# Second expert layer: one sum in DRAM, its accumulating scatters one at a time, copied straight to the output

## The chip, the cores and the metric

The kernel runs on one core of a Trainium2 chip. The metric is the device time of one execution in microseconds (us); lower is better. All spans below are from the first to the last instruction of that core.

## What is computed

A two-layer transformer on `x` of 2048 tokens by 128 channels, in f32. Layer 0 is an attention and a mixture of 64 experts, layer 1 is a lookup in place of attention and a mixture of 8 experts with two experts for each token. The change touches only the last of these:

```python
def _L1_ffn_ref(hidden_states, gate_w, gate_up_proj, down_proj):
    ...
    probs = jax.nn.softmax(x @ gate_w.T, axis=-1)
    w, idx = jax.lax.top_k(probs, TOP_K)              # TOP_K = 2 of E = 8
    w = w / jnp.sum(w, axis=-1, keepdims=True)
    combine = jnp.zeros((T, E), x.dtype).at[jnp.arange(T)[:, None], idx].add(w)
    def step(acc, inputs):
        gup, dn, ce = inputs
        g, u = jnp.split(x @ gup.T, 2, axis=-1)
        acc = acc + ce[:, None] * (jax.nn.silu(g) * u @ dn.T)
        return (acc, None)
...
x = x + _L1_ffn_ref(_layernorm(x, axis=-1), ...)
```

Each token's output row is its residual row `x` plus two weighted expert rows.

## The kernel before

The program is written by hand, engine by engine, with semaphores: SP issues the plain DMAs, PE multiplies, DVE and ACT move and transform, POOL (GpSimd) multiplies by masks in layer 0 and issues all indirect DMAs. Each engine and each queue runs its instructions in the order in which they are written.

The second expert layer is sparse. 4096 pairs of token and expert are sorted into slots of `slots_dram`, expert by expert, each expert's share filled up to whole tiles of 128 slots. There are at most 39 tiles (`TILES1`), and all 39 are always worked. A slot's row holds the normalised token (128 values), the number of its token (column `P`) and what gives its weight. An empty slot holds zeros and the number of a spare row behind the 2048 tokens.

- POOL L922 scatters the token rows into `slots_dram` (32 indirect DMAs).
- SP L378 loads tile j into `XG[j % 8]`. From tile 8 on it first waits until the scatter that read this buffer has landed (`summed0` or `summed1`, L377).
- PE turns the tile (L667), DVE copies it to `XTT` (L1226), ACT copies the expert's weights to `WB` (L825), PE multiplies gate and up (L679, 16 products of 128x128 by 128x128), ACT and DVE make the hidden values (L835, L1246), PE multiplies down (L689), and DVE weights the result into `YO[j % 4]` (`y_out`, L1233), which raises `y_taken`. From tile 4 on, `y_out` first waits until scatter j - 4 has landed (L1232).
- POOL L929 issues one indirect DMA for each tile: it adds the 128 rows of `YO` to the rows of a sum in DRAM that the token numbers name. There are two sums, `sums_dram[0]` for even tiles and `sums_dram[1]` for odd ones, each of 2048 + 128 rows. Scatter j waits for `y_taken` (L926) and for the landing of scatter j - 2 (L928), the last one on the same sum, since one token may occur in two tiles.
- Sum 0 starts as the residual `X` (SP L372, 1 MB, after the lookup), sum 1 as zeros (SP L326, 1088 KB, at the start of the program).
- At the end SP waits for both sums (L381), loads both in four quarters (L385, eight DMAs of 256 KB) into `X` and `BS`, DVE adds them quarter by quarter (L1258), and SP stores each quarter to `out` (L389).

The tiles on PE, DVE and ACT run some tiles ahead of the scatters, as far as `XG` (8), `YO` (4) and the pairs of other buffers allow.

Of the kernel before, what the change touches and what calls it, by code (L numbers as in the profile page):

```python
# [12 lines left out]
P = 128  # L13
T = 2048
NT = T // P
BANK = 512
CH = 512
NC = T // CH
# [14 lines left out]
TILES1 = (T * TOP1 + E1 * (P - 1)) // P  # L33
NXG = 8
# [73 lines left out]
def build(nc, a, out):  # L108

    f32, bf16, f32r, i32 = mybir.dt.float32, mybir.dt.bfloat16, mybir.dt.float32r, mybir.dt.int32  # L110
    ALU, ACT, AX = mybir.AluOpType, mybir.ActivationFunctionType, mybir.AxisListType
# [1 line left out]

    mask0_dram = nc.dram_tensor("mask0_scratch", (E0, T), f32, kind="Internal").ap()
    slots_dram = nc.dram_tensor("slots_scratch", (TILES1 * P, XW), f32, kind="Internal").ap()
    sums_dram = [nc.dram_tensor(f"sums_scratch{i}", (T + P, P), f32, kind="Internal").ap() for i in range(2)]

    ctx = ExitStack()
    with ctx:
        def sb(name, shape, dt=f32, stack=ctx):  # L120
            return stack.enter_context(nc.sbuf_tensor(name, shape, dt))
# [3 lines left out]
        def sem(name):  # L125
            if name not in sems:
                sems[name] = ctx.enter_context(nc.semaphore(name))
            return sems[name]
# [4 lines left out]
        X = sb("X", [P, NT, P])  # L133
# [22 lines left out]
        padrow = sb("padrow", [P, XW])  # L156
# [80 lines left out]
        sparse = ExitStack()  # L237
# [5 lines left out]
        YO = [sb(f"YO{i}", [P, P], f32, sparse) for i in range(4)]  # L243
        hits = sb("hits", [P, 2, E1], f32, sparse)
        wslot = sb("wslot", [P, 4], f32, sparse)
        BS = sb("BS", [P, NT, P], f32, sparse)
        sparse.close()

        lk = ExitStack()
# [52 lines left out]
        @block.sync  # L302
        def _(sp):
            def load(dst, src, name="loaded"):
                sp.dma_start(dst, src).then_inc(sem(name), 16)

            load(X[:, :, :], a["x"].rearrange("(t p) c -> p t c", p=P), "x_loaded")
            load(CF[:, :], a["consts"][:, 0:NF], "cf_loaded")
            load(YT[:, 0:NB], a["consts"][:, NF:NF + NB], "cb_loaded")
            load(wqk[:, :, :], a["wqk"], "qkv_loaded")  # L310
            load(bqk[:, :], a["bqk"], "qkv_loaded")
            load(wvt[:, :], a["wvt"], "qkv_loaded")
            load(bvb[:, :], a["bv"].partition_broadcast(P), "qkv_loaded")
            load(gam[:, :], a["gamma"].partition_broadcast(P), "rest_loaded")
            load(gw0[:, :], a["gw0"], "rest_loaded")
            load(gb0[:, :], a["gb0"].partition_broadcast(P), "rest_loaded")
            load(wol[:, :], a["wol"], "rest_loaded")
            load(bol[:, :], a["bol"].partition_broadcast(P), "rest_loaded")
            load(wout[:, :], a["wout"], "rest_loaded")
            load(boutb[:, :], a["bout"].partition_broadcast(P), "rest_loaded")  # L320
            load(gw1[:, :], a["gw1"], "rest_loaded")

            sp.wait_ge(sem("pad_ready"), 2)
            sp.dma_start(slots_dram.rearrange("(j p) c -> p j c", p=P),
                         padrow[:, :].unsqueeze(1).to_broadcast([P, TILES1, XW])).then_inc(sem("padded"), 16)
            sp.dma_start(sums_dram[1].rearrange("(t p) c -> p t c", p=P),  # L326
                         padrow[:, 0:P].unsqueeze(1).to_broadcast([P, NT + 1, P])).then_inc(sem("padded"), 16)
            sp.dma_start(sums_dram[0][T:T + P, :], padrow[:, 0:P]).then_inc(sem("padded"), 16)

            def load_weights(l, it, h, weights):  # L330
                sub = MOE[l]["sub"]
                sp.dma_start(WR[:, h * sub:(h + 1) * sub, :], weights[ds(it * 2 + h, 1)].squeeze(0)).then_inc(
                    sem(f"w_loaded{l}_{h}"), 16)

            def load_masks(l, it, h, mask_dram):
                k = it * 2 + h
                for s, p0, p1, e in SEGMENTS0:
                    sp.dma_start(MK[p0:p1, h, s, :], mask_dram[ds(k * 4 + e, 1), :].to_broadcast([p1 - p0, T])
                                 ).then_inc(sem(f"m_loaded{l}_{h}"), 16)

            def moe_loads(l, weights, mask_dram):

                m = MOE[l]
                sub, nb, npro, n = m["sub"], m["n_body"], m["n_pro"], m["halves"] // 2
                load_masks(l, 0, 0, mask_dram)
                load_masks(l, 0, 1, mask_dram)
                with sp.Fori(1, n) as it:
                    for h in range(2):
                        sp.wait_ge(sem(f"w_split{l}_{h}"), it * sub)
                        load_weights(l, it, h, weights)  # L350
                    for h in range(2):

                        sp.wait_ge(sem(f"h_ready{l}"), npro + (it - 1) * nb + (h + 1) * nb // 2)
                        load_masks(l, it, h, mask_dram)

                sp.sem_inc(sem(f"w_loaded{l}_0"), 16)


            sp.dma_start(WR[:, 2 * SUB0 - 2:2 * SUB0, :], a["wsh"]).then_inc(sem("wsh_loaded"), 16)
            load_weights(0, 0, 0, a["w0"])  # L360
            sp.wait_ge(sem("wsh_split"), 2)
            load_weights(0, 0, 1, a["w0"])
            sp.wait_ge(sem("mask_t0"), 4)
            sp.dma_start(mask0_dram[:, :], MT[0:E0, :]).then_inc(sem("mask_stored0"), 16)
            sp.wait_ge(sem("mask_stored0"), 16)
            moe_loads(0, a["w0"], mask0_dram)

            sp.wait_ge(sem("x_moe0"), NC)
            load(W1GU[:, :, :], a["w1gu"], "w1_loaded")
            load(W1D[:, :, :, :], a["w1d"], "w1_loaded")  # L370
            sp.wait_ge(sem("x_lookup"), 1)
            sp.dma_start(sums_dram[0][0:T, :].rearrange("(t p) c -> p t c", p=P), X[:, :, :]).then_inc(sem("x_kept"), 16)  # L372

            sp.wait_ge(sem("dispatched"), 16 * NT * TOP1)
            for j in range(TILES1):
                if j >= NXG:
                    sp.wait_ge(sem(f"summed{j % 2}"), 16 * ((j - NXG) // 2 + 1))  # L377
                sp.dma_start(XG[j % NXG][:, :], slots_dram[j * P:(j + 1) * P, :]).then_inc(sem(f"xg_loaded{j % NXG}"), 16)  # L378

            for i in range(2):  # L380
                sp.wait_ge(sem(f"summed{i}"), 16 * ((TILES1 + 1 - i) // 2))  # L381
            for q in range(NC):
                rows = slice(q * CH, (q + 1) * CH)
                for i, dst in ((0, X), (1, BS)):
                    sp.dma_start(dst[:, 4 * q:4 * q + 4, :], sums_dram[i][rows, :].rearrange("(t p) c -> p t c", p=P)  # L385
                                 ).then_inc(sem(f"sums_back{q}"), 16)
            for q in range(NC):
                sp.wait_ge(sem("x_final"), q + 1)
                sp.dma_start(out[q * CH:(q + 1) * CH, :].rearrange("(t p) c -> p t c", p=P),  # L389
                             X[:, 4 * q:4 * q + 4, :]).then_inc(sem("stored"), 16)  # L390
            sp.wait_ge(sem("stored"), 16 * NC)


# [447 lines left out]
        def _(pool):  # L841
# [72 lines left out]
                             ALU.add).then_inc(sem("xs_ready"), 1)  # L914
            norm_scale(3)

            pool.wait_ge(sem("padded"), 48)
            pool.wait_ge(sem("x_kept"), 16)
            pool.wait_ge(sem("rows_ready"), 3)
            for t in range(NT):  # L920
# [3 lines left out]

            for j in range(TILES1):
                pool.wait_ge(sem("y_taken"), j + 1)  # L926
                if j >= 2:
                    pool.wait_ge(sem(f"summed{j % 2}"), 16 * (j // 2))  # L928
                gp.indirect_dma_start(sums_dram[j % 2][:, :],  # L929
                                      bass.IndirectOffsetOnAxis(ap=XG[j % NXG][:, P:P + 1].bitcast(i32), axis=0),  # L930
                                      YO[j % 4][:, :], None, compute_op=ALU.add).then_inc(sem(f"summed{j % 2}"), 16)


        @block.vector
        def _(dve):
# [292 lines left out]
            def y_out(j):  # L1228

                dve.wait_ge(sem("y_done"), j + 1)  # L1230
                if j >= 4:
                    dve.wait_ge(sem(f"summed{j % 2}"), 16 * ((j - 4) // 2 + 1))  # L1232
                TS_(YO[j % 4][:, :], PS[:, (6 + j % 2) * BANK:(6 + j % 2) * BANK + P], wslot[:, j % 4:j % 4 + 1], None,  # L1233
                    ALU.mult).then_inc(sem("y_taken"), 1)

# [17 lines left out]
                    y_out(j - 1)  # L1253
            dve.wait_ge(sem("slot_weight"), TILES1)
            y_out(TILES1 - 1)
            for q in range(NC):
                dve.wait_ge(sem(f"sums_back{q}"), 32)
                TT(X[:, 4 * q:4 * q + 4, :], X[:, 4 * q:4 * q + 4, :], BS[:, 4 * q:4 * q + 4, :], ALU.add).then_inc(  # L1258
                    sem("x_final"), 1)


_OUT_SHAPE = (1, T, P)
# [54 lines left out]
```

## Time and profile before

| | us |
|---|---|
| three runs | 1236.63, 1236.97, 1242.84; median 1236.97 |
| the profiled execution's own time | 1237.94 |
| its span | 1236.1 |
| PE / DVE / ACT / POOL busy in it | 993.0 / 854.4 / 628.0 / 489.4 |
| scatters of the last stage, first to last start | 1114.94 to 1219.76, 39 of them |
| last landing to the end of the span | 1223.0 to 1236.1 |

The profile is one execution. Starts are counted from the start of the span. POOL's "busy" for an indirect DMA is the time in which it makes the descriptors; the transfer itself follows. When a transfer has landed is seen from the row of whoever waited for it.

### The profile page before, as it was taken

To read this page: it belongs to the slowest core of one execution; us is meant where nothing else is said; L and a number is where in the kernel's file an instruction comes from. 1 tells how busy PE (TensorE), PEld (TensorE's weight loads), DVE (VectorE), ACT (ScalarE), POOL (GpSimd) and SP (SyncE) were. 2 spreads that over 40 slices of the span, in tenths; PEclk is the share of its full clock that TensorE was granted. 3 is DMA by queue.
4 is the path that set the end of the run, shared out by engine and by line. 5 is a ranking of instruction groups with operands and counts; after the bars stand their busy time and mean duration, and the time that the engine had idled before them with its cause. 6 is when DMAs were issued, how large, how long until landed. Compare 5 with 4: busy or idle time off the path is not lost.

```text
span 1236.1 us, 18848 instructions
## 1 busy us (share of the span) xinstructions
PE 993.0 (80%) x6540; PEld 621.8 (50%) x6540; DVE 854.4 (69%) x1310; ACT 628.0 (51%) x839; POOL 489.4 (40%) x346
## 2 busy tenths in 40 slices
PE   4344999999999935999999999999963675029993
PEld 2112222222222324877777777777743335029993
DVE  5789999999999865776677767776766334204442
ACT  1330888888888721555655555555531100115551
POOL 4000000000000041788888888888851001545553
PEclk9655999999999967999999999999985576559997
DMA  5600000000000003657564576545313001123335
GB/s 135 124 1 1 1 2 1 2 1 2 1 2 2 1 20 85 156 126 185 138 156 121 135 178 142 149 121 142 81 68 136 0 1 34 36 60 45 51 52 117
DMA packets 41101, 86.87 MB, mean 70 GB/s; under 512 B 5009, under 2 KB 30993, under 8 KB 34577
## 3 DMA queue, kind: packets, MB, share of 16 engines
q1 hardware_dynamic: 34400, 81.11, 26.0%
q0 software_dynamic: 6640, 4.94, 2.9%
q8 instruction: 41, 0.67, 0.2%
q14 instruction: 20, 0.16, 0.0%
HBM read 74.40 MB, written 11.63 MB: 70 GB/s over the span
## 4 chain that ended last, share of the span: by engine, by line
PE 42%; POOL 20%; DVE 17%; issue 12%; ACT 6%; DMA 2%; POOLq 1%; SPq 0%; ACTq 0%; DVEq 0%
POOL HF L894 14%; PE PS L499 11%; PE PS L486 6%; PE PS L476 6%; PE PS L679 6%; DVE HL L1091 4%; PE PS L689 3%; POOL slots_scratch L922 2%; POOL WL L863 2%; ACT HH L776 2%; DVE small L1011 1%; DVE hm L994 1%; ACT PB L744 1%; PE PS L417 1%; DVE XN L953 1%
## 5 line engine op out<-in xcount | busy, mean ns | idle before, releaser
L744 ACT ACTIVATE PB<-PS 128x1024 f32<-128x1024 f32 x256 | 261.8, 1024 | 92.0 <-PE PS L486 81.9
L1032 DVE TENSOR_SCALAR PS<-PS 128x1024 f32<-128x1024 f32 x256 | 302.7, 1228 | 7.6 <-PE PS L476 2.7
L894 POOL TENSOR_TENSOR HF<-SU,MK 128x512 f32<-128x512 f32 x192 | 283.6, 1497 | 60.1 <-DVE SU L1098 60.1
L1091 DVE TENSOR_TENSOR HL<-HF,HH 128x512 fp32r<-128x512 f32 x200 | 188.4, 942 | 119.0 <-ACT HH L776 118.7
L846 POOL TENSOR_SCALAR rstd<-moments 128x16 f32<-128x16 f32 x4 | 1.0, 261 | 535.9 <-DVE moments L949 535.9
L776 ACT CAST HH<-HF 128x512 fp32r<-128x512 f32 x200 | 124.2, 621 | 168.0 <-POOL HF L894 155.7
L499 PE MATMUL PS<-PB,VS 128*32 128x256 f32 x2048 | 164.3, 393 | 0.6 <-ACT PB L744 0.5
L567 PE MATMUL PS<-XH,WL 128*128 128x512 f32 x400 | 162.3, 406 | 0.0
L569 PE MATMUL PS<-XH,WH 128*128 128x512 f32 x400 | 157.5, 394 | 0.0
L568 PE MATMUL PS<-XL,WH 128*128 128x512 f32 x400 | 156.6, 391 | 0.0
L1098 DVE TENSOR_TENSOR SU<-PS,SL 128x512 f32<-128x512 f32 x200 | 135.7, 678 | 13.0 <-ACT SL L783 12.9
L783 ACT ACTIVATE SL<-PS 128x512 f32<-128x512 f32 x200 | 118.7, 593 | 37.1 <-PE PS L569 36.1
L476 PE MATMUL PS<-QS,KP 64*128 64x512 bf16 x512 | 100.1, 388 | 5.1 <-DVE QM L1028 2.9
L486 PE MATMUL PS<-QM,KP 64*128 64x512 bf16 x512 | 100.9, 391 | 1.0 <-DVE PS L1032 0.9
L567 PEld LDWEIGHTS PS<-XH,WL 128*128 128x128 f32 x400 | 75.0, 188 | 33.4 <-DVE SU L1098 15.5
L929 POOL DMA_INDIRECT sums_scratch<-YO,XG x39 | 60.8, 1558 | 59.3 <-DVE YO L1233 56.8
L569 PEld LDWEIGHTS PS<-XH,WH 128*128 128x128 f32 x400 | 75.2, 188 | 17.9
L551 PE MATMUL PS<-HL,WH 128*128 128x512 f32 x200 | 82.5, 413 | 1.1 <-DVE HL L1091 1.1
L568 PEld LDWEIGHTS PS<-XL,WH 128*128 128x128 f32 x400 | 75.3, 188 | 13.7
L549 PE MATMUL PS<-HH,WL 128*128 128x512 f32 x200 | 79.1, 396 | 1.0 <-ACT HH L776 1.0
L1226 DVE COPY XTT<-PS 128x128 f32<-128x128 f32 x39 | 11.4, 292 | 98.6 <-PE PS L667 53.1
L552 PE MATMUL PS<-HH,WH 128*128 128x512 f32 x200 | 79.1, 396 | 0.0
(212 smaller groups left out, 1253.7 us busy)
## 6 DMA issues: line engine op xcount, KB each, us to landing
MK<-mask_scratch SPq DMA_DIRECT2D x32, 768.0 KB, 11.8
MK<-mask_scratch SPq DMA_DIRECT2D x32, 512.0 KB, 9.2
WR<-in_w SPq DMA_DIRECT2D x16, 576.0 KB, 4.5
MK<-mask_scratch SPq DMA_DIRECT2D x32, 256.0 KB, 9.8
W1GU<-in_w1gu SPq DMA_DIRECT2D x1, 4096.0 KB, 12.1
slots_scratch<-padrow SPq DMA_DIRECT2D x1, 2827.5 KB, 20.2
XG<-slots_scratch SPq DMA_DIRECT2D x39, 72.5 KB, 1.9
W1D<-in_w1d SPq DMA_DIRECT2D x1, 2048.0 KB, 17.3
```

What stands on the lines that cost most here:

```text
L476: last = mm(bank(2 * (u % 3) + k), KP[g][hp][r, n * P:(n + 1) * P], QS[g][r, c * CH:(c + 1) * CH], start=True, stop=True)
L486: last = mm(bank(2 * (u % 3) + k), KP[g][hp][r, n * P:(n + 1) * P], QM[g][r, c * CH:(c + 1) * CH], start=False, stop=True, skip_group_chec ...
L499: last = mm(PS[32 * j:32 * j + 32, at + q.start:at + q.stop], VS[:, n, g * HG + j, :], PB[u // 2 % 3][:, 2 * (j % 2) + j // 2, q], start=( ...
L567: mm(o, WL[:, slot, w], XH[:, x], start=True, stop=False)
L568: mm(o, WH[:, slot, w], XL[:, x], start=False, stop=False)
L569: last = mm(o, WH[:, slot, w], XH[:, x], start=False, stop=True)
L744: A(PB[u // 2 % 3][:, 2 * hp:2 * hp + 2, :], pair_banks(u).rearrange("p (j q) -> p j q", j=2), ACT.Exp).then_inc(sem("exp_done"), 1)
L776: nc.scalar.copy(HH[buf][:, :], HF[buf % 2][:, :]).then_inc(sem(f"hh_ready{l}"), 1)
L894: ins = gp.tensor_tensor(HF[k % 2][:, :], SU[k % 2][:, :], mask, ALU.mult)
L1032: TS_(pair_banks(u), pair_banks(u), 4.0, 0.0, ALU.mult, ALU.max).then_inc(sem("relu_done"), 1)
L1091: TT(HL[buf][:, :], HF[buf % 2][:, :], HH[buf][:, :].bitcast(f32), ALU.subtract).then_inc(sem(f"hl_ready{l}"), 1)
L1098: TT(SU[k % 2][:, :], bank(2 * (k % 2) + 1), SL[k % 2][:, :], ALU.mult).then_inc(sem(f"su_done{l}"), 1)
```

## The change

Both sums become one, `sums_dram`, with 2048 + 128 rows that start as the residual `X`. Its scatters share one semaphore, `summed`, and scatter j waits for the landing of scatter j - 1 rather than of scatter j - 2. The zeroing of sum 1 and its buffer `BS` go. At the end neither loads nor additions are left: after the last scatter has landed, SP issues four DMAs from the sum in DRAM straight to `out` in DRAM.

```diff
-    sums_dram = [nc.dram_tensor(f"sums_scratch{i}", (T + P, P), f32, kind="Internal").ap() for i in range(2)]
+    sums_dram = nc.dram_tensor("sums_scratch", (T + P, P), f32, kind="Internal").ap()
...
-        BS = sb("BS", [P, NT, P], f32, sparse)
...
-            sp.dma_start(sums_dram[1].rearrange("(t p) c -> p t c", p=P),
-                         padrow[:, 0:P].unsqueeze(1).to_broadcast([P, NT + 1, P])).then_inc(sem("padded"), 16)
-            sp.dma_start(sums_dram[0][T:T + P, :], padrow[:, 0:P]).then_inc(sem("padded"), 16)
+            sp.dma_start(sums_dram[T:T + P, :], padrow[:, 0:P]).then_inc(sem("padded"), 16)
...
-            sp.dma_start(sums_dram[0][0:T, :].rearrange("(t p) c -> p t c", p=P), X[:, :, :]).then_inc(sem("x_kept"), 16)
+            sp.dma_start(sums_dram[0:T, :].rearrange("(t p) c -> p t c", p=P), X[:, :, :]).then_inc(sem("x_kept"), 16)
...
                 if j >= NXG:
-                    sp.wait_ge(sem(f"summed{j % 2}"), 16 * ((j - NXG) // 2 + 1))
+                    sp.wait_ge(sem("summed"), 16 * (j - NXG + 1))
...
-            for i in range(2):
-                sp.wait_ge(sem(f"summed{i}"), 16 * ((TILES1 + 1 - i) // 2))
+            sp.wait_ge(sem("summed"), 16 * TILES1)
             for q in range(NC):
                 rows = slice(q * CH, (q + 1) * CH)
-                for i, dst in ((0, X), (1, BS)):
-                    sp.dma_start(dst[:, 4 * q:4 * q + 4, :], sums_dram[i][rows, :].rearrange("(t p) c -> p t c", p=P)
-                                 ).then_inc(sem(f"sums_back{q}"), 16)
-            for q in range(NC):
-                sp.wait_ge(sem("x_final"), q + 1)
-                sp.dma_start(out[q * CH:(q + 1) * CH, :].rearrange("(t p) c -> p t c", p=P),
-                             X[:, 4 * q:4 * q + 4, :]).then_inc(sem("stored"), 16)
+                sp.dma_start(out[rows, :], sums_dram[rows, :]).then_inc(sem("stored"), 16)
...
-            pool.wait_ge(sem("padded"), 48)
+            pool.wait_ge(sem("padded"), 32)
...
                 pool.wait_ge(sem("y_taken"), j + 1)
-                if j >= 2:
-                    pool.wait_ge(sem(f"summed{j % 2}"), 16 * (j // 2))
-                gp.indirect_dma_start(sums_dram[j % 2][:, :],
+                if j >= 1:
+                    pool.wait_ge(sem("summed"), 16 * j)
+                gp.indirect_dma_start(sums_dram[:, :],
...
-                                      YO[j % 4][:, :], None, compute_op=ALU.add).then_inc(sem(f"summed{j % 2}"), 16)
+                                      YO[j % 4][:, :], None, compute_op=ALU.add).then_inc(sem("summed"), 16)
...
                 if j >= 4:
-                    dve.wait_ge(sem(f"summed{j % 2}"), 16 * ((j - 4) // 2 + 1))
+                    dve.wait_ge(sem("summed"), 16 * (j - 3))
...
-            for q in range(NC):
-                dve.wait_ge(sem(f"sums_back{q}"), 32)
-                TT(X[:, 4 * q:4 * q + 4, :], X[:, 4 * q:4 * q + 4, :], BS[:, 4 * q:4 * q + 4, :], ALU.add).then_inc(
-                    sem("x_final"), 1)
```

No instruction changes its place on PE or ACT. On POOL's queue, the first scatters of the second expert layer stand like this before (out<-in with buffer numbers, then what each waits for):

```order
L929 DMA sums_scratch0<-YO0,XG0 2176x128 [waits y_taken]
L929 DMA sums_scratch1<-YO1,XG1 2176x128 [waits y_taken]
L929 DMA sums_scratch0<-YO2,XG2 2176x128 [waits summed0,y_taken]
L929 DMA sums_scratch1<-YO3,XG3 2176x128 [waits summed1,y_taken]
L929 DMA sums_scratch0<-YO0,XG4 2176x128 [waits summed0,y_taken]
```

and like this after the change:

```order
L919 DMA sums_scratch<-YO0,XG0 2176x128 [waits y_taken]
L919 DMA sums_scratch<-YO1,XG1 2176x128 [waits summed,y_taken]
L919 DMA sums_scratch<-YO2,XG2 2176x128 [waits summed,y_taken]
L919 DMA sums_scratch<-YO3,XG3 2176x128 [waits summed,y_taken]
L919 DMA sums_scratch<-YO0,XG4 2176x128 [waits summed,y_taken]
```

The scatters are as many and in the same order; each now waits for its direct neighbour. On SP's queue, the end of the program before:

```order
L378 DMA XG6<-slots_scratch 128x145 [waits summed0]
L385 DMA X<-sums_scratch0 128x4x128 [waits summed1,summed0]
L385 DMA BS<-sums_scratch1 128x4x128
L385 DMA X<-sums_scratch0 128x4x128
L385 DMA BS<-sums_scratch1 128x4x128
L385 DMA X<-sums_scratch0 128x4x128
L385 DMA BS<-sums_scratch1 128x4x128
L385 DMA X<-sums_scratch0 128x4x128
L385 DMA BS<-sums_scratch1 128x4x128
L389 DMA out_0<-X 128x4x128 [waits x_final] x4
```

and after:

```order
L375 DMA XG6<-slots_scratch 128x145 [waits summed]
L380 DMA out_0<-sums_scratch 16x4096 [waits summed]
L380 DMA out_0<-sums_scratch 16x4096 x3
```

Twelve DMAs and four waits for DVE become four DMAs behind one wait.

## Rows read from the trace of the kernel before

**Rows 1.** Chain that ended last, in order of time: start us, length us, whose work.

```profile
1204.22 1.79 PE PS L679 x16
1207.01 1.79 PE PS L679 x16
1209.80 1.79 PE PS L679 x16
1212.56 4.60 DMA sums_scratch<-YO,XG
1217.89 1.56 POOL sums_scratch L929
1219.76 3.23 DMA sums_scratch<-YO,XG
1226.23 0.96 SPq L385
1227.23 5.44 DMA BS<-sums_scratch
```

**Rows 2.** Windows of PE and clock: start:end, length, busy by engine, PEclk, DMA, GB/s.

```profile
core 0: us, PE busy (x) PEld busy (x) DVE busy (x) ACT busy (x) POOL busy (x), PEclk, DMA share, GB/s
62.00:124.00 62.00, 27.70 (x220) 11.51 (x220) 53.59 (x42) 12.62 (x9) 0.00 (x0) 0.50 0.00 1
...
1010.00:1030.00 20.00, 13.63 (x75) 10.55 (x73) 8.24 (x21) 0.00 (x0) 0.00 (x0) 0.90 0.11 33
1105.50:1109.40 3.90, 3.90 (x19) 3.90 (x19) 0.46 (x3) 0.61 (x2) 0.00 (x0) 0.50 0.34 76
1114.00:1212.50 98.50, 98.50 (x885) 98.50 (x884) 48.21 (x179) 57.49 (x70) 54.53 (x35) 1.00 0.37 48
```

**Rows 3.** POOL's scatters in time: start, length, in brackets idle before and its releaser.

```profile
1114.94 1.62 POOL L929 DMA_INDIRECT sums_scratch<-YO,XG  x1 [13.67 <-DVE YO L1233]
...
1137.25 1.55 POOL L929 DMA_INDIRECT sums_scratch<-YO,XG  x1 [1.23 <-DVE YO L1233]
1140.04 1.56 POOL L929 DMA_INDIRECT sums_scratch<-YO,XG  x1 [1.24 <-DVE YO L1233]
1142.83 1.55 POOL L929 DMA_INDIRECT sums_scratch<-YO,XG  x1 [1.23 <-DVE YO L1233]
1145.62 1.56 POOL L929 DMA_INDIRECT sums_scratch<-YO,XG  x1 [1.24 <-DVE YO L1233]
1148.41 1.55 POOL L929 DMA_INDIRECT sums_scratch<-YO,XG  x1 [1.23 <-DVE YO L1233]
...
1217.89 1.56 POOL L929 DMA_INDIRECT sums_scratch<-YO,XG  x1 [1.92 <-DMA sums_scratch<-YO,XG]
1219.76 1.56 POOL L929 DMA_INDIRECT sums_scratch<-YO,XG  x1 [0.30 <-issue]
```

**Rows 4.** SP's queue in time: the five tile loads that wait for those scatters.

```profile
1140.57 0.32 SPq L378 DMA_DIRECT2D XG<-slots_scratch  x1
1144.49 0.32 SPq L378 DMA_DIRECT2D XG<-slots_scratch  x1
1146.16 0.32 SPq L378 DMA_DIRECT2D XG<-slots_scratch  x1
1148.99 0.32 SPq L378 DMA_DIRECT2D XG<-slots_scratch  x1
1151.64 0.32 SPq L378 DMA_DIRECT2D XG<-slots_scratch  x1
```

**Rows 5.** DVE in time, one weighting of a tile (L1233).

```profile
1142.21 0.34 DVE L1233 TENSOR_SCALAR YO<-PS,wslot 128x128 f32<-128x128 f32 x1
```

**Rows 6.** Line L679, products of gate and up: ns min/median/max.

```profile
L679 PE MATMUL PS<-XTT,WB x624: 274/275/542, 1105.5 to 1214.1; 128*128 128x128 f32 x156
```

**Rows 7.** DMA issues by form: KB each, median us from issue to landing.

```profile
XG<-slots_scratch SPq DMA_DIRECT2D x39, 72.5 KB, 1.9
...
sums_scratch<-X SPq DMA_DIRECT2D x1, 1024.0 KB, 5.1
```

**Rows 8.** SP's queue in time at the end of the program: start, length.

```profile
1223.00 0.37 SPq L385 DMA_DIRECT2D X<-sums_scratch  x1
1223.41 0.51 SPq L385 DMA_DIRECT2D BS<-sums_scratch  x1
```

**Rows 9.** SP's queue in time at the start of the program.

```profile
24.61 10.47 SPq L326 DMA_DIRECT2D sums_scratch<-padrow  x1
35.12 8.68 SPq L328 DMA_DIRECT2D sums_scratch<-padrow  x1
43.84 0.43 SPq L359 DMA_DIRECT2D WR<-in_wsh  x1
```

**Rows 10.** Tile WR: who reads the weights, first and last start us.

```profile
L752 ACT CAST WH<-WR x53: 506/508/512, 434.4 to 905.0; 128x384 fp32r<-128x384 f32 x53
```

## The prediction, made before the changed kernel ran

> **What bounds the kernel now.** I read the chain of waits first, because it tells which work ended last and what released it. Up to 1211.6 us it is nothing but the gate and up products of PE (L679), one group for each tile [rows 1]. They start 2.79 us apart (1207.01 less 1204.22), though a group is 1.79 us long: the missing 1.00 us is the turning of a later tile and the down products, which PE does in between. The windows confirm it: from 1114.0 to 1212.5 PE is busy 98.5 of 98.5 us at a granted clock of 1.00 [rows 2]. The stage of the second expert layer is bound by PE at 2.79 us a tile.
>
> The scatters are the second thing to look at, since the change puts them closer together in what they wait for. POOL starts one every 2.79 us, and before each it idled 1.23 us until DVE had weighted the tile [rows 3]. So POOL follows PE and has 1.23 us to spare. What a scatter costs as a whole is not its 1.56 us on POOL, which is descriptor making, but the time until it has landed. Five tile loads on SP tell it, because each waits for exactly one scatter eight tiles back: scatters that started at 1137.25, 1140.04, 1142.83, 1145.62 and 1148.41 [rows 3] let loads start at 1140.57, 1144.49, 1146.16, 1148.99 and 1151.64 [rows 4]. The differences are 3.32, 4.45, 3.33, 3.37 and 3.23 us, 3.54 on the mean. A scatter thus lands 3.3 us after its start, sometimes a microsecond later, and is still in flight when the next one starts at +2.79. With two sums that is allowed: scatter j waits only for scatter j - 2, started 5.58 us before.
>
> The tail is third. The last tiles come faster than the rest, and there the chain passes over to the scatters [rows 1]. The last one starts at 1219.76 and lands at 1222.99; from there to the end of the span at 1236.1 stand 13.1 us of loading both sums, adding and storing.
>
> **Part 1: scatter j waits for scatter j - 1.** This adds 37 waits that can last (the ones of scatters 2 to 38 move up by one) and one that did not exist (scatter 1). The period can no longer be below landing plus the time that POOL needs to start again. The landing is 3.54 us, above. The restart has one row: in the tail, scatter 37 waited for the landing of scatter 35, which came at 1212.56 + 4.60 = 1217.16, and it started at 1217.89 [rows 1]. That is 0.73 us. The period is then 3.54 + 0.73 = 4.27 us, above PE's 2.79, so the chain of scatters takes the lead from the second scatter on. There are 38 periods between the first start and the last. The first start stays at 1114.94, because it waits for nothing new. Last start: 1114.94 + 38 x 4.27 = 1277.2 us, against 1219.76 before. **Cost: 57.5 us.**
>
> Bounds of the period. Below: the last scatter, with nothing behind it, landed after 3.23 us [rows 1], and the nearest row for a quicker restart is the one after DVE's signal: the weighting ended at 1142.55 [rows 5] and the scatter started at 1142.83 [rows 3], 0.28 us. Together 3.51 us, a cost of 28.6 us. With the measured restart of 0.73 the low end is 3.96, a cost of 45.7. Above: the pair in the tail, 1217.89 less 1212.56 = 5.33 us from start to start, if every landing were as late as that one; a cost of 97.7. I take 4.27, because the landings are measured five times in the same stage and the restart is after a landing, as it will be in the changed kernel.
>
> What is queued behind the waiting POOL instruction: only further scatters. Who waits for them: DVE's `y_out` (four tiles back) and SP's tile loads (eight back). DVE stalls in `y_out(j)` until scatter j - 4 has landed, and that carries the slow pace to DVE, PE and ACT. It does not cost a second time. When scatter j - 4 lands, `YO` of tiles j - 3 to j - 1 is ready already, so POOL always finds its next tile. The loads of `XG` do not take the lead either: a load takes 1.9 us [rows 7], and the tile that it brings is turned for DVE before the next scatter lands 4.27 us later.
>
> **Part 2: the tail.** Removed are eight loads of 256 KB, four additions and four stores: 13.1 us from landing to end. Added are four DMAs of 256 KB from DRAM to DRAM. The trace shows none of that kind, so I bound it. The eight loads, 2 MB, were issued from 1223.00 [rows 8] and the last landed at 1227.23 + 5.44 = 1232.67 [rows 1], so half as much takes 4.8 us: the lower end, reading alone. The store of 1 MB of `X` into the sum took 5.1 us [rows 7]. Reading and writing one after the other would be 9.9, and three further issues at 0.5 us each [rows 8] make 11.4: the upper end. I take 5.1 + 1.5 = 6.6 us, since a copy reads and writes at the same time. **Gain: 13.1 - 6.6 = 6.5 us** (1.7 to 8.3).
>
> **Part 3: the start.** The zeroing of sum 1 occupied SP's queue for 10.47 us; the next loads on the queue are weights [rows 9] that nobody reads before 434.4 us [rows 10], while the queue is through at 44. Taking it away gains nothing. Its cover is 390 us deep.
>
> **Sum.** The span becomes 1236.1 + 57.5 - 6.5 = 1287.1 us. Around the span the profiled execution has 1237.94 - 1236.1 = 1.8 us, which gives 1288.9. That execution was 1.0 us above the median of the three runs, so the forecast for a median is **1288 us**. As a formula: time = 1125.7 + 38 x period.
>
> **PE's clock in the slower stage** is what could multiply the cost. At 2.79 of 4.27 us PE will be busy 65% of the time. The rows point both ways. Between 62 and 124 us PE was busy 27.70 of 62 us and had 1.2 GHz (granted 0.50); between 1010 and 1030 us it was busy 13.63 of 20 us (68%) and had 2.4 GHz most of the time (0.90); and at the start of this stage, dense work at 0.50 from 1105.50 to 1109.40 was followed by 1.00 [rows 2]. At 0.50 one product takes 542 ns against 275 [rows 6], so a tile would take 2 x 2.79 = 5.58 us and PE would be the bound again. But then PE has no idle time at all, which is the state after which the clock rose at 1109.4, and the three tiles that wait in `YO` cover a few slow tiles. I expect spells at 0.50 that cost little.
> The Trainium skill, TensorE: Matmul & The Clock Gate, section "HAM oscillation — how this bites in real kernels", describes this very shape: short bursts of matmuls with a DMA wait after each put the array back to half clock in every round. By that rule, if it held all the time, the period would be 5.58 and not 4.27; the trace agrees only for stretches much emptier than 65%.
>
> **Rivals.**
> 1. PE at half clock sets the pace: 5.58 us a tile, 1125.7 + 38 x 5.58 = 1337.7 us. For it: the row at 62 to 124 us. Against it: the 68% row, and that the state ends itself.
> 2. Every landing is late. Scatter 35 needed 4.60 us [rows 1] and scatter 9 needed 4.45. If this is the rule once a scatter touches the rows that the one before has just written, the period is 5.33 and the time 1328 us. Against it: those two also ran beside a neighbour, and four of five landings took 3.23 to 3.37.
> 3. POOL restarts in 0.28 us rather than 0.73, and a lone scatter lands in 3.23: 3.51 us, 1259 us. For it: the last scatter. Against it: the only restart after a landing is 0.73.
> 4. Not slower: a scatter that has the queue to itself lands so much sooner that PE hides it. It decides at a period of (1237.0 - 1125.7) / 38 = 2.93 us, so a landing of 2.93 - 0.73 = 2.20 us; with PE's 2.79 the time would be 1125.7 + 106.0 = 1231.7 us. Against it: POOL alone takes 1.56 us for the descriptors, and no row shows a landing below 3.2.
> The Trainium skill, DMA: Bandwidth & Descriptors, section "Latency and other measured facts", says that a lighter load on HBM makes the fixed cost of a DMA smaller; if so the landing would be nearer to 3.23 than to 3.54, and the sum 1288 - 38 x 0.31 = 1276 us. The last scatter (3.23 us) agrees weakly.
>
> **Chances.** Forecast, with periods of 3.9 to 4.9 us: 80%. Rival 1: 5%; rival 2: 5%; rival 3 (and what lies between it and the forecast): 8%; rival 4: 2%. The range goes from a period of 3.9 (1274 us) to one of 4.9 (1312 us), which holds the bounds of the tail's cost around a typical period too. A measurement of this kernel can tell about 0.5% from no change, 6 us. Only rival 4 comes near that: faster 1%, same 1%, slower 98%.
>
> **What would show it.** POOL's scatters start some 4.27 us apart, each with about 2.7 us of idle time before it, ended by the DMA on `sums_scratch` instead of DVE. Most of the chain of waits in the last stage changes from PE L679 to that DMA. PE is busy about 65% of the stage. The tail from last landing to end is about 6.6 us, without DVE. All spans before 1114 us are unchanged. The forecast is wrong if the period is not landing plus restart: if idle time before the scatters is still ended by DVE (then PE is the bound, and its clock says which rival), or if the restart is not 0.7.

## The result

The changed kernel takes 1282.6 us (median of four runs, 1273.9 to 1288.0) against 1239.5 us for the kernel before on the same chip (1236.6 to 1242.8). The ratio is 1.034, with a 95% interval of 1.027 to 1.041: it is slower by 43 us. The profiled execution of the changed kernel took 1273.85 us, the quickest of the four.

The page of the changed kernel, its head and its chain by line (to be held against the span and the chain of [rows 1]):

```profile
span 1272.0 us, 18835 instructions
...
PE 33%; POOL 19%; DVE 17%; issue 13%; DMA 10%; ACT 5%; POOLq 1%; DVEq 0%; ACTq 0%; SPq 0%
```

DMA now has 10% of the chain, where the page of the kernel before gave it 2%; PE fell from 42% to 33%. The end of the chain in order of time (start, length, whose work) shows what the 10% are:

```profile
1245.81 3.33 DMA sums_scratch<-YO,XG
...
1249.88 3.26 DMA sums_scratch<-YO,XG
1253.14 0.02 issue
1253.16 0.02 POOLq L918
1253.18 0.69 issue
1253.87 3.25 DMA sums_scratch<-YO,XG
...
1257.86 3.27 DMA sums_scratch<-YO,XG
```

Where [rows 1] had one PE group every 2.79 us there is now one scatter every 4.0 us, and between the end of one (1249.88 + 3.26 = 1253.14) and the start of the next (1253.87) the same 0.73 us that the prediction took from a single row (POOLq L918 is POOL's wait for the landing, in an instruction of its own). POOL in time (start, length, idle before and its releaser) answers [rows 3]:

```profile
1108.32 1.62 POOL L919 DMA_INDIRECT sums_scratch<-YO,XG  x1 [13.42 <-DVE YO L1223]
1112.44 1.59 POOL L919 DMA_INDIRECT sums_scratch<-YO,XG  x1 [2.50 <-DMA sums_scratch<-YO,XG]
1116.51 1.56 POOL L919 DMA_INDIRECT sums_scratch<-YO,XG  x1 [2.48 <-DVE YO L1223]
...
1261.86 1.55 POOL L919 DMA_INDIRECT sums_scratch<-YO,XG  x1 [2.45 <-DMA sums_scratch<-YO,XG]
```

From first to last start are 1261.86 - 1108.32 = 153.5 us, or 4.04 us a period, against 104.8 us before. The line's own view says how long a scatter takes to land, and who is named for the waits:

```profile
  DVE YO L1223: 87.8, 31
  DMA sums_scratch<-YO,XG: 20.0, 8
...
DMA to landing us min/median/max: 3.2/3.3/3.8
```

The first two rows have to be read with care. They give 87.8 of 107.8 us of POOL's idle time to DVE, as if PE and DVE were still ahead of POOL. They are not. DVE in the same stretch (1180 to 1182 us), then POOL:

```profile
1180.53 0.35 DVE L1223 TENSOR_SCALAR YO<-PS,wslot 128x128 f32<-128x128 f32 x1 [1.54 <-DMA sums_scratch<-YO,XG]
```

```profile
1181.14 1.55 POOL L919 DMA_INDIRECT sums_scratch<-YO,XG  x1 [2.37 <-DVE YO L1223]
```

DVE itself had waited 1.54 us for a scatter. One landing released both: DVE to weight a tile four further on, and POOL to scatter a tile that had long been weighted. DVE's signal came 0.26 us before POOL started, so it is the last one that came, and the view names it. The period tells which is the true releaser, and the length of the scatter's landing with it: after the last weightings, where DVE has nothing left to signal, the scatters still start 4.0 us apart, and there the view names the DMA (1261.86 above).

The end of the program on SP's queue answers [rows 8]:

```profile
1265.18 2.49 SPq L380 DMA_DIRECT2D out<-sums_scratch  x4
```

The last scatter landed at 1265.17, and the span ended at 1272.0: a tail of 6.8 us against 13.1.

The spans of the two traces now add up: 153.5 - 104.8 = +48.7 us for the scatters, 6.8 - 13.1 = -6.3 us for the tail, and -6.6 us because the first scatter started at 1108.3 instead of 1114.9. Together +35.8, and 1272.0 - 1236.1 = 35.9. The last of the three terms is not the change's. POOL's last multiplication by a mask in layer 0 starts at 911.9 us in one trace and at 911.4 in the other, so 6.1 of the 6.6 us arise after it, where both kernels have the same instructions up to the first scatter. In the lookup stage that follows, PE was granted a clock of 0.58 on the mean in one trace and 0.68 in the other. Windows of the kernel before and, below, of the changed one (columns as in [rows 2]):

```profile
918.00:1020.00 102.00, 59.36 (x165) 32.66 (x164) 48.75 (x89) 11.70 (x10) 7.65 (x3) 0.58 0.15 62
```

```profile
918.00:1020.00 102.00, 58.64 (x204) 32.88 (x204) 49.60 (x91) 11.71 (x10) 7.65 (x3) 0.68 0.15 62
```

The times of the four runs of the changed kernel go the same way as their clocks: spans of 1272.0, 1277.9, 1283.5 and 1286.1 us at a mean granted clock of 0.885, 0.881, 0.872 and 0.873. The two kernels' runs are spread over 6 and 14 us, so periods and tails from the traces are sharper than the times.

### The profile page after: what moved, and what is told of

It reads as the page before. It is cut to its first block, busy times and chain, and to the rows that moved or that the text cites. A ratio compares the mean times of both kernels' runs of the same rounds, so it can differ in the third digit from the quotient of the medians.

```text
span 1272.0 us, 18835 instructions
## 1 busy us (share of the span) xinstructions
PE 1001.0 (79%) x6540; PEld 620.9 (49%) x6540; DVE 853.6 (67%) x1306; ACT 628.4 (49%) x839; POOL 489.7 (38%) x346
## 4 chain that ended last, share of the span: by engine, by line
PE 33%; POOL 19%; DVE 17%; issue 13%; DMA 10%; ACT 5%; POOLq 1%; DVEq 0%; ACTq 0%; SPq 0%
POOL HF L884 14%; PE PS L489 11%; DMA sums_scratch<-YO,XG 9%; PE PS L476 6%; PE PS L466 6%; DVE HL L1081 4%; POOL slots_scratch L912 2%; POOL WL L853 2%; ACT HH L766 2%; DVE small L1001 1%; DVE hm L984 1%; ACT PB L734 1%; PE PS L407 1%; DVE XN L943 1%; DVE stats L936 1%
## 5 line engine op out<-in xcount | busy, mean ns | idle before, releaser
L919 POOL DMA_INDIRECT sums_scratch<-YO,XG x39 | 60.8, 1558 | 107.7 <-DVE YO L1223 87.8
L669 PE MATMUL PS<-XTT,WB 128*128 128x128 f32 x624 | 79.5, 282 | 1.0 <-issue 0.5
```

## The experiments

All kernels below are built from one of the two; the diff is against the one named. "Period" is the distance of the first from the last scatter's start, divided by 38.

### The waits alone

```diff
 (kernel before)
-                if j >= 2:
-                    pool.wait_ge(sem(f"summed{j % 2}"), 16 * (j // 2))
+                if j >= 1:
+                    pool.wait_ge(sem(f"summed{(j - 1) % 2}"), 16 * ((j + 1) // 2))
```

> The kernel before with the waits alone changed: two sums, the old tail, but scatter j waits for scatter j - 1. Theory (period = landing + restart of POOL): 3.30 + 0.73 = 4.0 us from scatter to scatter, 153 us from the first start to the last against 104.8 before, tail 13.1 us as before, so about 49 us slower than before (1288 us). Rival (a landing is late because the scatter adds to rows that its neighbour has just written, which two sums avoid): landings clearly below the 3.3 us of the changed kernel, period below 3.8 us, less than 40 us slower.

Measured: 1291.5 us (1286.1 to 1294.3), ratio 1.042 (1.037 to 1.047) to the kernel before. The line of the scatters in its trace:

```profile
L929 POOL DMA_INDIRECT sums_scratch<-YO,XG x39: 1553/1558/1617, 1119.0 to 1273.5; - x39
...
DMA to landing us min/median/max: 3.2/3.3/4.4
```

The period is (1273.5 - 1119.0) / 38 = 4.07 us, and the landing 3.3 us with two sums as with one. So the waits alone cost everything: 154.5 - 104.8 = +49.7 us in the trace, +55.0 in the medians (in the trace the first scatter also came 4.1 us later than before, which these waits cannot do). That neighbours add to the same rows plays no part in the landing; the rival falls.

### The tail alone

```diff
 (kernel before)
-                for i, dst in ((0, X), (1, BS)):
-                    sp.dma_start(dst[:, 4 * q:4 * q + 4, :], sums_dram[i][rows, :]...).then_inc(sem(f"sums_back{q}"), 16)
-            for q in range(NC):
-                sp.wait_ge(sem("x_final"), q + 1)
-                sp.dma_start(out[q * CH:(q + 1) * CH, :]..., X[:, 4 * q:4 * q + 4, :]).then_inc(sem("stored"), 16)
+                sp.dma_start(out[rows, :], sums_dram[0][rows, :]).then_inc(sem("stored"), 16)
...
-            for q in range(NC):
-                dve.wait_ge(sem(f"sums_back{q}"), 32)
-                TT(X[...], X[...], BS[...], ALU.add).then_inc(sem("x_final"), 1)
```

> The kernel before with the tail alone changed: four copies from DRAM to DRAM in place of eight loads, four additions and four stores. It leaves out the addition of sum 1, so the output lacks the odd tiles. Theory: scatters stay 2.79 us apart, and the tail from last landing to end is 6.9 us against 13.1, so 6 us faster than before (1233 us). Rival (copies from DRAM to DRAM were only so quick because little else was left in flight after the slow scatters): tail above 9 us, gain below 4 us.

Measured: 1234.9 us (1226.7 to 1236.0) against 1236.5 on that chip, ratio 0.997 (0.994 to 0.9997). SP and POOL at the end of its trace:

```profile
1218.94 2.49 SPq L384 DMA_DIRECT2D out<-sums_scratch  x4
```

```profile
1215.64 1.56 POOL L923 DMA_INDIRECT sums_scratch<-YO,XG  x1 [0.31 <-issue]
```

From the copies' issue at 1218.94 to the end of its span at 1225.5 are 6.6 us, after scatters at the old pace. The tail's gain of 6.5 us does not hang on the slow scatters. The times show less of it (1.6 us between medians), and their spread of 9 us is wider than the term itself; the trace is the better witness for the size.

### The order of POOL's two waits

```diff
 (changed kernel)
-                pool.wait_ge(sem("y_taken"), j + 1)
                 if j >= 1:
                     pool.wait_ge(sem("summed"), 16 * j)
+                pool.wait_ge(sem("y_taken"), j + 1)
```

> The changed kernel with POOL's two waits before each scatter written the other way round (landing first, then the weighted tile). Theory A (the 0.71 us between landing and restart are the price of a separate waiting instruction ahead of the DMA): the restart falls to about 0.3 us, the period from 4.04 to 3.6 us, 16 us faster than the changed kernel (about 1266 us). Theory B (the restart costs that much after any landing): period and time unchanged (4.04 us, 1280 us).

Measured: 1260.8 us (1259.4 to 1262.0), ratio 1.018 (1.014 to 1.022) to the kernel before. The two swapped lines are worth 22 us of median, or some 20 by the two ratios, since the kernel before was 3 us quicker on this chip. In the trace:

```profile
L919 POOL DMA_INDIRECT sums_scratch<-YO,XG x39: 1553/1558/1617, 1111.6 to 1248.5; - x39
...
  DMA sums_scratch<-YO,XG: 75.7, 37
...
DMA to landing us min/median/max: 3.1/3.3/4.6
```

The period is 136.9 / 38 = 3.60 us with the landing as before, so the restart fell from 0.73 to 0.27 us. Theory A holds. The instructions in the two traces show what differs: of the two waits written ahead of the scatter, the first is carried by the DMA instruction (L919) and the second becomes an instruction of its own in front of it (L918). In the changed kernel the separate one waits for the landing, and 0.69 us pass between its end and the DMA's start (the rows of 1253.16 and 1253.18 above). Here the DMA instruction itself waits for the landing, and L918 is the wait for the weighted tile. The scatter started at 1237.92 landed at 1241.09, and the chain goes on:

```profile
1241.12 0.02 POOLq L918
1241.14 0.22 issue
1241.35 1.55 POOL sums_scratch L919
```

What POOL does in the 0.69 us no row shows. This term costs 38 x 0.44 = 16.6 us of the changed kernel's 48.7, and the view now names the true releaser too (75.7 us to the DMA).

### What the addition costs

```diff
 (changed kernel)
-                                      YO[j % 4][:, :], None, compute_op=ALU.add).then_inc(sem("summed"), 16)
+                                      YO[j % 4][:, :], None).then_inc(sem("summed"), 16)
```

> The changed kernel with scatters that overwrite instead of add (the output is then not the sum). It prices the addition inside the landing. Theory (most of the landing is descriptor making, 1.56 us, and the fixed way to DRAM and back): landing 3.1 to 3.3 us, period 3.8 to 4.0 us. Rival (the addition, a read of DRAM before the write, is a large part of the landing): landing below 2.8 us, period below 3.5 us.

Measured in a single run: 1245.8 us.

```profile
L919 POOL DMA_INDIRECT sums_scratch<-YO,XG x39: 957/958/962, 1114.0 to 1235.0; - x39
...
DMA to landing us min/median/max: 2.2/2.2/4.3
```

My expectation was wrong and the rival right: an overwriting scatter lands in 2.2 us, an adding one in 3.3. Of the 1.1 us, 0.60 is descriptor making on POOL (958 against 1558 ns), the rest is in flight. Even so the period stays above 2.79 us in most places (2.97 in the median, 121.0 / 38 = 3.18 on the mean), so that with this order of waits a serial chain would hold this kernel even without the addition. With the restart of 0.27 us it would be 2.2 + 0.27, an estimated 2.5 us, and PE would be the bound again; no run has both. The longest landing, 4.3 us, also says that a late landing needs neither the addition nor a second scatter in flight.

### The zeroing put back

```diff
 (changed kernel)
+    zeroed = nc.dram_tensor("zeroed", (T + P, P), f32, kind="Internal").ap()
...
+            sp.dma_start(zeroed.rearrange("(t p) c -> p t c", p=P),
+                         padrow[:, 0:P].unsqueeze(1).to_broadcast([P, NT + 1, P])).then_inc(sem("padded"), 16)
...
-            pool.wait_ge(sem("padded"), 32)
+            pool.wait_ge(sem("padded"), 48)
```

> The changed kernel with the zeroing DMA of 1088 KB put back at the start of the program, into a tensor that nobody reads. Theory (the zeroing is hidden behind 390 us of other work, and the 6.6 us by which the changed kernel's first scatter starts earlier come from the clock that PE was granted, not from the change): period 4.04 us, tail 6.8 us, time of the changed kernel, 1274 to 1288 us, and a first scatter anywhere between 1108 and 1119 us. Rival (taking the zeroing away brought the 6.6 us): first scatter at 1115 us or later, time some 6 us above the changed kernel.

Measured: 1281.1 us (1275.0 to 1286.6), next to 1282.6 (1273.9 to 1288.0) without the zeroing. Its first scatter started at 1115.8 us. That single start would also fit the rival, but the medians do not, though four runs spread over 12 to 14 us could hide a few microseconds. Starts vary as much among kernels that share the zeroing: 1119.0 with the waits alone, 1114.9 before, 1111.6 with the tail alone. The kernel with the swapped waits has no zeroing and starts at 1111.6 as well. And the zeroing is over in the first 50 us, while 6.1 of the 6.6 us arose after 911 us. The zeroing costs nothing that can be seen.

### Less work for PE, with one sum and with two

```diff
 (changed kernel, and kernel before)
-                for k in range(I1 // P):
+                for k in range(1):
                     last = mm(o, HT[j % 2][:, k * P:(k + 1) * P], W1D[:, ds(expert, 1), k, :].squeeze(1),
-                              start=(k == 0), stop=(k == I1 // P - 1))
+                              start=True, stop=True)
```

> The changed kernel with one of the four down products of each tile (it leaves out three quarters of the hidden values), so PE has less to do in each tile. Theory (scatters alone set the pace): period 4.0 us as with all the products. Rival (PE still takes part in the pace): period shorter by some tenths of a microsecond.

> The kernel before with the same cut. Theory (PE sets the pace there): the period falls from 2.79 us to 2.2 or 2.3, not below 2.0, half of landing plus restart, where its own pairs of scatters would hold. Rival (the scatters already held the kernel before): period unchanged at 2.79.

Measured in a single run each: 1275.9 us with one sum, 1232.5 us with two. The scatters with one sum, then with two:

```profile
L919 POOL DMA_INDIRECT sums_scratch<-YO,XG x39: 1553/1557/1616, 1110.3 to 1264.2; - x39
```

```profile
L929 POOL DMA_INDIRECT sums_scratch<-YO,XG x39: 1554/1558/1617, 1119.1 to 1214.0; - x39
```

With one sum the period is 153.9 / 38 = 4.05 us, as with the full work: PE has no part in it. With two sums the 104.8 us become 94.9, a period of 2.54 us in the even stretches. PE did hold the kernel before, but the gain is smaller than expected. The down products fell from 1.06 to 0.39 us a tile, and the period only by 0.25, because PE now waits for DVE to copy the turned tile:

```profile
1161.84 2.05 PE L679 MATMUL PS<-XTT,WB 128*128 128x128 f32 x16 [0.16 <-DVE XTT L1226]
```

So between 2.79 and 2.5 us a tile a second bound lies close below PE's, which the prediction did not need but a next change would meet.

### An attempt at the tail of the kernel before

```diff
 (kernel before; POOL's two waits also in the order of the third experiment)
-            for i in range(2):
-                sp.wait_ge(sem(f"summed{i}"), 16 * ((TILES1 + 1 - i) // 2))
-            for q in range(NC):
-                rows = slice(q * CH, (q + 1) * CH)
-                for i, dst in ((0, X), (1, BS)):
+            for i, dst in ((1, BS), (0, X)):
+                sp.wait_ge(sem(f"summed{i}"), 16 * ((TILES1 + 1 - i) // 2))
+                for q in range(NC):
+                    rows = slice(q * CH, (q + 1) * CH)
                     sp.dma_start(dst[:, 4 * q:4 * q + 4, :], sums_dram[i][rows, :]...).then_inc(sem(f"sums_back{q}"), 16)
```

> The kernel before, whole, with sum 1 loaded as soon as its own last scatter has landed (four loads, 1.7 us before the last scatter of sum 0 lands), only the four loads of sum 0 left behind the last landing, and POOL's two waits written in the order that restarted it sooner. Theory (the tail is bound by eight loads behind one wait): tail 9 to 10 us instead of 13.1, and 0.4 us less in the last scatters, 3 to 4 us faster than before (1233 us). Rival (DMA engines are the bound, and the same 2 MB take as long): tail above 12 us, no change.

Measured: 1237.7 us (1231.6 to 1241.1) against 1238.3, ratio 0.9992 (0.997 to 1.0015): no difference that these runs can tell.

```profile
1217.12 2.05 SPq L384 DMA_DIRECT2D BS<-sums_scratch  x4
1219.21 3.35 SPq L384 DMA_DIRECT2D X<-sums_scratch  x4
```

```profile
1213.81 3.29 DMA sums_scratch<-YO,XG
...
1220.91 5.88 DMA X<-sums_scratch
```

The loads of sum 1 did start 2.1 us earlier than those of sum 0, but the last load of sum 0, issued at 1220.91, still took 5.9 us to land. The last scatter landed at 1219.0, and from there to the end at 1230.5 are 11.5 us, 1.6 less than before. It lies between the theory (9 to 10) and the rival (above 12), which suggests that what is moved counts as well as what is waited for; no run separates the two. I have no version that beats the kernel before by more than can be measured.

## Why the prediction held, step by step

**The bound and who takes it over: right.** PE held the kernel before (less work for PE made it quicker), and with one sum the chain of landing plus restart holds it (less work for PE changed nothing). The waits alone reproduce the whole loss.

**The period: 4.27 us predicted, 4.04 measured.** The restart of 0.73 us was right to the hundredth (median; 0.74 on the mean of 38), though it came from a single row; the term that was too large is the landing. I took 3.54 us, the mean of five in which one had 4.45; in the changed kernel the mean is 3.30, the median 3.27 and the longest 3.77. The kernel with the tail alone tells what landings are at the old pace, with a neighbour in flight:

```profile
DMA to landing us min/median/max: 3.2/3.3/5.0
```

The mean of its 39 is 3.43 us. So about half of the error is a sample of five with one late landing in it, and half is that late landings became rarer (above 3.6 us: 5 of 39 there, 2 of 39 in the changed kernel). They did not disappear (4.4 us once in the trace of the waits alone), and what makes a landing late stays open. The surplus of 0.23 us a period makes 38 x 0.23 = 8.7 us. The forecast lies only 5.4 us above the measured 1282.6, because something else went the other way: it was built on a median of 1237.0 us for the kernel before, which was 1239.5 in the comparison. That part is luck.

**Bounds and rival 3.** The low end used a restart of 0.28 us from the row after DVE's signal, and I called it unlikely after a landing. For the changed kernel as written that was right. But the two numbers were not a matter of who signals: they differ by which instruction carries the wait. With the waits swapped, the restart after a landing is 0.27 us, and the kernel comes to 1260.8 us, where rival 3 had 1259.

**The tail: right in its sum.** 6.6 us predicted, 6.8 measured (6.6 with the tail alone). The terms were each a little off and cancelled: the last of the four copies was issued 1.9 us after the first (1.5 in the prediction) and landed 4.4 us later (5.1), and about 0.5 us from there to the end had no term.

**The start: right**, as the zeroing put back shows. But "all spans before 1114 us are unchanged" was wrong as a statement on one trace: the first scatter came 6.6 us early, most of it in the lookup stage with its higher clock, and I should have given the time ahead of the stage a spread of its own.

**PE's clock in the stage: its premise was off, the outcome right.** I worked with 65% busy. The window says otherwise:

```profile
1108.30:1244.00 135.70, 116.55 (x907) 106.17 (x906) 51.54 (x181) 57.26 (x71) 53.00 (x34) 0.99 0.26 34
```

PE is busy 116.55 of 135.7 us, 86%, at 0.99. I had divided 2.79 us of work by the period, but one tile's work takes longer when it stands alone. Turning, down, and gate and up of one tile in the changed kernel:

```profile
1182.30 0.33 PE L657 MATMUL PS<-CF,XG 128*128 128x128 f32 x1 [0.58 <-DMA XG<-slots_scratch]
1182.51 1.15 PE L679 MATMUL PS<-W1D,HT 128*128 x8
1183.68 2.02 PE L669 MATMUL PS<-XTT,WB 128*128 128x128 f32 x16
```

From 1182.30 to 1185.70 are 3.40 us; before, the ends of the groups overlapped with the starts of the next, and 2.79 us held all of them. So the clock was never near the sparse stretches that rival 1 needed, and the spells at 0.50 that I expected did not come. The kernel with one sum and less work for PE comes nearer to the 65% (86.90 of 120 us, 72%), and it too was granted 0.97:

```profile
1120.00:1240.00 120.00, 86.90 (x601) 74.90 (x602) 44.54 (x156) 50.66 (x63) 45.10 (x29) 0.97 0.26 35
```

The Trainium skill, TensorE: Matmul & The Clock Gate, section "HAM oscillation — how this bites in real kernels", which the prediction quoted, describes DMA waits that are longer than the bursts between them. Here the idle times of PE before a tile were 0.1 to 1.7 us between bursts of 3.4 us, and the trace does not show the fall to half clock in every round: the prediction was wrong to call it this very shape.

**Rival 2** (late landings as a rule) and **rival 4** (a lone scatter lands so soon that PE hides it) fell with the landing at 3.3 us. The prediction also quoted the Trainium skill, DMA: Bandwidth & Descriptors, section "Latency and other measured facts", on a fixed cost that falls with the load. That may be seen in the mean (3.30 us against 3.43 at the old pace), not in the quickest landings (3.2 in both).

**What would show it** had one wrong sign: I wrote that idle time before the scatters would be ended by the DMA and that DVE's name there would refute the forecast. The view names DVE in 31 of 39 cases, and the forecast holds.

## What to carry to other kernels

Accumulators that exist only so that two transfers can be in flight are worth their merge at the end when landing plus restart exceeds the pace of the work by enough over all transfers: here 4.04 us against 2.79, 38 times, cost 49 us where the merge costs 6.5. Where a chain of landings cannot be avoided, write the wait that comes last as the one that the DMA instruction itself carries; that was worth 16.6 us of the trace here, and 20 to 22 of the times, yet at 3.60 us a period it did not make up for the second sum. And when two engines wait for the same landing, a view that names the last signal can name the bystander: compare the period with landing plus restart before believing it.

## What the hardware showed that I had not expected

- A wait in an instruction of its own ahead of an indirect DMA on POOL makes the restart 0.73 us; carried by the DMA it is 0.27 us.
- An adding scatter of 128 rows of 512 bytes costs 1.1 us more until landing than an overwriting one (3.3 against 2.2 us), of which 0.60 us is descriptor making.
- Adding to rows that the scatter before has just written is no slower than adding to other rows (3.3 us with one sum and with two).
- In a stage in which PE is busy a little over half of the time, the same instructions got a mean clock of 0.58 in one execution and 0.68 in another, and of the 6.6 us between their first scatters 6.1 arose from this stage on.
